# A gated attention and expert-bias block: two buffers for the turned score blocks, the router's rows turned on TensorE, x moved in halves from ScalarE's queue

## The reference, cut to what matters

```python
x = x + tanh(g_xattn) * xattn(_layernorm(x), ctx, mask, Wq, bq, Wk, bk, Wv, bv, Wo, bo)
x = x + tanh(g_ffn)   * ffn(_layernorm(x), router_weight, router_bias, expert_bias)
# xattn: x is (8, 512, 2048); each batch is cut along s into 16 patches of 512 x 128
q, k = Wq @ patch(ln(x)) + bq, Wk @ patch(ln(x)) + bk      # 256 x 128 per patch
v    = Wv @ patch(ctx) + bv
attn = softmax(q_h^T k_h / sqrt(32) masked)                # 8 heads, 128 x 128 each
out  = (Wo @ gelu(attn v^T) + bo) * mask
# ffn: rows t of 2048 features, 64 experts
scores = softmax(flat @ router_weight^T + bias); keep the 8 largest, w_dense
out = flat * sum(kept) + w_dense @ expert_bias
```

## Time and profile before

| | |
|---|---|
| time, median of 3 runs | 1323.04 us (1320.9 to 1323.36) |
| profiled execution, its own time | 1328.39 us |
| its span | 1326.4 us |
| mean granted TensorE clock | 0.963 |
| busy: PE, DVE, ACT, POOL | 85%, 73%, 76%, 66% of the span |
| DMA traffic | 232.27 MB, mean 175 GB/s |

### The profile page before, as it was taken

The page is one execution under the profiler, slowest core; times in us unless marked ns, Lnnn a source line. Parts: engine busy times, 40 slices in busy tenths (PEclk is TensorE's granted clock), DMA queues, the critical chain, the costliest instruction groups (busy, mean ns, idle before and its releaser), DMA issues.

```text
span 1326.4 us, 32364 instructions
## 1 busy us (share of the span) xinstructions
PE 1123.9 (85%) x11165; PEld 1010.7 (76%) x11165; DVE 968.2 (73%) x1859; ACT 1004.8 (76%) x3072; POOL 871.4 (66%) x784
## 2 busy tenths in 40 slices
PE   3779899888898888897888899898989879889857
PEld 3668788878887777787877788787878778878745
DVE  6647768877589766888578876788658876688546
ACT  4767788877789588787879778887778858888743
POOL 2457778567785577856776678756777557775631
PEclk9899999999999899999999999989999989999979
DMA  9395555796557955588656966579555795557543
GB/s 275 105 209 143 137 139 144 182 291 154 143 138 215 259 131 144 141 268 214 147 140 145 290 182 149 135 194 281 144 144 137 229 250 132 143 135 220 138 109 127
DMA packets 169763, 232.27 MB, mean 175 GB/s; under 512 B 27776, under 2 KB 104704, under 8 KB 169472
## 3 DMA queue, kind: packets, MB, share of 16 engines
q1 hardware_dynamic: 168736, 230.19, 66.3%
q10 hardware_dynamic: 864, 0.01, 0.0%
HBM read 80.06 MB, written 33.65 MB: 86 GB/s over the span
## 4 chain that ended last, share of the span: by engine, by line
SPq 36%; DVE 18%; PE 12%; DMA 10%; ACT 10%; issue 9%; POOL 5%; DVEq 0%; ACTq 0%; POOLq 0%
SPq L551 33%; DMA PT<-T 8%; ACT P L643 7%; DVE T L797 5%; DVE T L806 2%; POOL ht_lo L1118 2%; DVE X L936 2%; DVE o L812 2%; DVE nmx L790 2%; DMA cx<-in_ctx 1%; ACT L643 1%; PE ring L475 1%; SPq L556 1%; PE ring L343 1%; DVE bnst L946 1%
## 5 line engine op out<-in xcount | busy, mean ns | idle before, releaser
L643 ACT ACTIVATE P<-ring,nmx 128x128 f32<-128x128 f32 x1024 | 360.6, 389 | 2.1 <-DVE nmx L790 1.3
L328 PE MATMUL ring<-z_hi,wqk_hi 128*128 128x256 f32 x1024 | 302.1, 295 | 24.8 <-DVE z_lo L1000 21.1
L329 PE MATMUL ring<-z_hi,wqk_lo 128*128 128x256 f32 x1024 | 294.3, 287 | 0.0
L330 PE MATMUL ring<-z_lo,wqk_hi 128*128 128x256 f32 x1024 | 294.1, 287 | 0.0
L797 DVE STREAM_TRANSPOSE T<-P 128x512 f32<-128x512 f32 x256 | 170.8, 687 | 135.9 <-DMA PT<-T 134.9
L1106 POOL TENSOR_TENSOR X<-X,xt 128x512 f32<-128x512 f32 x128 | 165.2, 1291 | 153.1 <-DVE xt L825 152.1
L1118 POOL TENSOR_TENSOR ht_lo<-PT,ht_hi 128x512 fp32r<-128x512 f32 x124 | 160.1, 1292 | 133.7 <-ACT ht_hi L667 133.5
L643 ACT ACTIVATION_READ_ACCUMULATOR P<-ring,nmx 128x1 f32 x1024 | 234.5, 229 | 0.0
L328 PEld LDWEIGHTS ring<-z_hi,wqk_hi 128*128 128x128 f32 x1024 | 200.9, 196 | 38.9 <-DVE wqk_lo L975 21.1
L643 ACT ACT_TABLE_LOAD x62 | 79.5, 1283 | 171.0 <-DVE nmx L790 171.0
L825 DVE SCALAR_TENSOR_TENSOR xt<-ring,cst,mg 128x256 f32<-128x256 f32 x256 | 111.5, 477 | 131.3 <-PE ring L405 131.0
(11 more groups left out here) (139 smaller groups left out, 2806.9 us busy)
## 6 DMA issues: line engine op xcount, KB each, us to landing
PT<-T SPq DMA_DIRECT2D x992, 112.0 KB, 2.3
cx<-in_ctx SPq DMA_DIRECT2D x128, 256.0 KB, 3.8
out_y<-X SPq DMA_DIRECT2D x128, 256.0 KB, 4.4
X<-in_x SPq DMA_DIRECT2D x112, 256.0 KB, 4.9
mg<-in_mask SPq DMA_DIRECT2D x64, 128.0 KB, 3.8
X<-in_x SPq DMA_DIRECT2D x8, 512.0 KB, 7.5
sel<-rows_d SPq DMA_DIRECT2D x256, 3.0 KB
PT<-T SPq DMA_DIRECT2D x32, 80.0 KB, 2.6
```

Of the source, the lines that this page charges most:

```text
L328: e.matmul(o, wqk_hi[:, t, cols], z_hi[:, t, :], t == 0, False)
L329: e.matmul(o, wqk_lo[:, t, cols], z_hi[:, t, :], False, False)
L330: last = e.matmul(o, wqk_hi[:, t, cols], z_lo[:, t, :], False, t == DT - 1)
L643: last = e.activation(P[:, n, :], bank("S", 4 * u + g)[:, k * W:(k + 1) * W], ACT.Exp, bias=nmx[u % 2][:, n:n + 1], accum_out=den[u % 2][: ...
```

## The change

It does five things. T becomes two buffers of 20 blocks and PT one of 20; `turn_p(u)` and `turn_d(u)` wait for the moves of u-2 to have landed instead of u-1, and `move(u)` no longer waits for anything of the router. For all units X is turned by `r_turn` on TensorE into two PSUM banks; `r_high` copies from there (ScalarE) and `r_low` subtracts on VectorE; GpSimd has no part in it. `o32` has two buffers, not three. Loads and stores of x are 512 KB (half a tile), 8 and 8 per batch, issued by ScalarE between its activations; only batch 1's first load (16 of 256 KB) and the last batch's stores stay on SP. The tail of a batch is no longer put off by `late` (14.75 slots), and every slot is new.

```diff
-    rows=-11.5, z32=-25.5, z_hi=-20, z_lo=-14.75, q=-14.5, q_ev=-5.25, k=-11, k_ev=-7.5,
-    S=-1.25, top=4, exp=3.5, e_gap=0.25, tp=7, td=7.75, mv=7.25, PV=20, on=23.5,
-    mix=43, m_gap=0.75,
...
+    rows=-26, z32=-25.25, z_hi=-16.75, z_lo=-21.25, q=-12.5, q_ev=-1.75, k=-9, k_ev=-6.75,
+    S=-0.75, top=3.5, exp=4, e_gap=0.25, tp=6.25, td=8, mv=8.75, PV=21.5, on=23.5,
+    mix=42.25, m_gap=0.25,
+    sx=44, sx_gap=1, x2=43.25, st=45.25, st_gap=0.75, rl=50, rl_gap=3.5,
...
-        NC, NV, NR, NO = 2, 4, 7, 3
+        NC, NV, NR, NO = 2, 4, 7, 2
...
-        T = sb("T", [128, 4, 28, 32])
-        PT = sb("PT", [128, 4, 28, 32])
+        T = [sb(f"T{i}", [128, 4, 20, 32]) for i in range(2)]
+        PT = sb("PT", [128, 4, 20, 32])
...
                 for a in range(2):
                     for u in units(t, "hT", C["hT_gap"] * a):
-                        if u >= TF0:
-                            r_turn(u, a)
-                    for u in due(t, C["t_R"] + C["t_gap"] * a, count=TF0):
+                        r_turn(u, a)
+                    for u in units(t, "R", C["hT_gap"] * a):
                         r_mm(u, a)
...
                 if u:
                     e.wait_ge(on_v, u)
-                if u > HLAG:
-                    e.wait_ge(htlo_g, 2 * (u - HLAG))
-                n = 28 if u >= HLAG else 20
-                if u >= HLAG:
-                    e.wait_ge(turn_v, u - HLAG + 1)
                 for b in range(4):
                     for a in range(4):
-                        e.dma_start(PT[32 * b:32 * b + 32, a, 0:n, :], T[32 * a:32 * a + 32, b, 0:n, :]).then_inc(pt_in, 16)
+                        e.dma_start(PT[32 * b:32 * b + 32, a, :, :], T[u % 2][32 * a:32 * a + 32, b, :, :]).then_inc(pt_in, 16)
...
         @block.scalar
         def _(e):
+            def store(b, t, h):
+                e.wait_ge(x2_v, (b * DT + t) * 4 + 2 * h + 2)
+                e.dma_start(ov[b, t, :, h * 1024:(h + 1) * 1024], X[b % 2][:, t, h * 1024:(h + 1) * 1024]).then_inc(out_done[t], 16)
+
+            def load_x(b, t, h):
+                e.wait_ge(out_done[t], out_value(b - 2))
+                e.dma_start(X[b % 2][:, t, h * 1024:(h + 1) * 1024],
+                            xv[b, t, :, h * 1024:(h + 1) * 1024]).then_inc(x_in[b % 2][t], 16)
...
-                if u < TF0:
-                    e.wait_ge(pt_in, 256 * (u + HLAG + 1))
-                    e.activation(by_block(ht_hi[a][:]), turned(a), ACT.Copy).then_inc(hthi_a, 1)
-                else:
-                    e.wait_ge(ht_pe, n - 2 * TF0 + 1)
-                    e.activation(by_block(ht_hi[a][:]), blocks(bank("hT", n)[:]), ACT.Copy).then_inc(hthi_a, 1)
+                e.wait_ge(ht_pe, n + 1)
+                e.activation(ht_hi[a][:], bank("hT", n)[:], ACT.Copy).then_inc(hthi_a, 1)
...
             def turn_p(u, g):
-                if u:
-                    e.wait_ge(pt_in, 256 * u)
+                if u >= 2:
+                    e.wait_ge(pt_in, 256 * (u - 1))
...
-            def turn_h(u):
-                e.wait_ge(pt_in, 256 * (u + HLAG))
-                b, c = divmod(u, NU)
-                e.wait_ge(x1_g, 2 * (u + 1))
-                e.transpose(T[:, :, 20:28, :].rearrange("p q (w t) i -> p w q t i", w=2),
-                            X[b % 2][:, :, c * U:(c + 1) * U].rearrange("p t (w q i) -> p w q t i", w=2, q=4)).then_inc(turn_v, 1)
-
             def r_low(u, a):
                 n = 2 * u + a
...
+                e.tensor_tensor(ht_lo[a][:], bank("hT", n)[:], f32(ht_hi[a][:]), ALU.subtract).then_inc(htlo_v, 1)
```

More of the change, by code:

```diff
@@ L235, in batch @@
             return due(t, 128 + lag, 128, NB)
-        def after(t, lag):
-            return due(t, 128 + lag + C["late"], 128, NB - 1) + tuple(b for b in due(t, 128 + lag, 128, NB) if b == NB - 1)
         def o_parts(u):
@@ L290, in gated_block_kernel @@
                 for u in units(t, "hT", C["hT_gap"] * a):
-                    if u >= TF0:
-                        take(("hT", 2 * u + a), t, end("ht_lo", u) - end("hT", u), htlo_v, 2 * (u - TF0) + a + 1)
-            for b in after(t, C["LT"]):
+                    take(("hT", 2 * u + a), t, end("ht_lo", u) - end("hT", u), htlo_v, 2 * u + a + 1)
+            for b in batch(t, C["LT"]):
                 take(("LT", b), t, C["c_top"] - C["LT"], lg_v, b + 1)
-            for b in after(t, C["wT"]):
+            for b in batch(t, C["wT"]):
                 take(("wT", b), t, C["wt_lo"] - C["wT"], wtlo_v, b + 1)
             for i in range(16):
-                for b in after(t, C["mix"] + C["m_gap"] * i):
+                for b in batch(t, C["mix"] + C["m_gap"] * i):
                     take(("mix", b * 16 + i), t, C["x2"] - C["mix"], x2_v, b * 16 + i + 1)
@@ L593, in _ @@
                 for i in range(16):
-                    for b in after(t, C["x2"] + C["m_gap"] * i):
-                        store(b, i // 4, i % 4)
-                    for b in after(t, C["rl"] + C["rl_gap"] * i):
-                        if b + 2 < NB:
-                            load_x(b + 2, i // 4, i % 4)
+                    for b in batch(t, C["x2"] + C["m_gap"] * i):
+                        if b == NB - 1:
+                            store_last(i // 4, i % 4)
                 for i in due(t, C["x_1"], C["x_gap"], 16):
@@ L603, in _ @@
                         e.wait_ge(v_m, V_SW)
-                    load_x(1, i // 4, i % 4)
+                    load_x1(i // 4, i % 4)
             for t in range(DT):
@@ L675, in c_logits @@
                 e.wait_ge(r_pe, 2 * NU * (b + 1))
-                e.activation(blocks(L[:]), by_block(PR[:]), ACT.Copy).then_inc(l_a, 1)
+                e.activation(L[:], PR[:], ACT.Copy).then_inc(l_a, 1)
             def c_exp(b):
@@ L760, in _ @@
                 for a in range(2):
-                    for u in due(t, C["t_hi"] + C["t_gap"] * a, count=TF0):
+                    for u in units(t, "ht_hi", C["hT_gap"] * a):
                         r_high(u, a)
-                    for u in units(t, "ht_hi", C["hT_gap"] * a):
-                        if u >= TF0:
-                            r_high(u, a)
-                for b in after(t, C["L"]):
+                for b in batch(t, C["L"]):
                     c_logits(b)
-                for b in after(t, C["c_exp"]):
+                for b in batch(t, C["c_exp"]):
                     c_exp(b)
-                for b in after(t, C["wt_hi"]):
+                for b in batch(t, C["wt_hi"]):
                     w_high(b)
                 for i in range(DT):
-                    for b in after(t, C["sx"] + C["sx_gap"] * i):
+                    for b in batch(t, C["sx"] + C["sx_gap"] * i):
                         scale_x(b, i)
+                for i in range(8):
+                    for b in batch(t, C["st"] + C["st_gap"] * i):
+                        if b < NB - 1:
+                            store(b, i // 2, i % 2)
+                    for b in batch(t, C["rl"] + C["rl_gap"] * i):
+                        if b + 2 < NB:
+                            load_x(b + 2, i // 2, i % 2)
         @block.vector
@@ L1066, in _ @@
                     w_low(b)
-                for b in after(t, C["c_sc"]):
+                for b in batch(t, C["c_sc"]):
                     if b < NB - 1:
@@ L1157, in _ @@
                         add_x(u, j)
-                for a in range(2):
-                    for u in due(t, C["t_lo"] + C["t_gap"] * a, count=TF0):
-                        r_low(u, a)
                 for b in batch(t, C["norm2"]):
```

84 lines of the change are left out of this document (27 added, 57 removed), and 10 rows, old and new, of the table ENDS.

## The result

The changed kernel takes 1314.5 us (median of 4 runs, 1311.48 to 1316.57), the one before 1323.2 us beside it (1320.9 to 1323.88): the ratio is 0.9935, 95% interval 0.9912 to 0.9959. It is faster by 0.7%, 8.7 us, where 22 us were forecast. The profiled execution took 1316.57 us, with a span of 1314.7.

The account below looks back on a forecast made before the run. A ring of dependences, with one buffer T waiting for landings, bounded the kernel. After the change a batch takes 8 x 17.3 + 15.0 = 153.4 against 156.2 us; over 7.9 batches 22 us less, so 1301 us, range 1252 to 1340.

Parts of the forecast that it names:

- The ordinary unit: Any unit outside a batch's tail, timed between neighbouring units' moves: 17.9 us before, forecast 17.3 us after the change.
- the ring that was named: Chain through four engines from one unit's `o_high` to the next one's, with half of `project_out` added: 17.3 us.
- The other ring, of PT: Single buffer PT: issues, landing, `weigh`, `divide`, reciprocal and turn of the denominators, put at 16.1 us a unit, not deciding.
- Turns of X on TensorE, cost nothing: Eight transposes a unit start within 0.84 us; TensorE busy 16.5 us, under 17.3, so cost nothing.
- Rival D: Slower by TensorE: transposes take 0.275 us each, 17.9 us a unit, 158.2 a batch, 1339 us; chance 0.07.
- Router's parts, SP, third buffer: VectorE gains two subtractions, at most 11.1 us busy, covered; SP's ctx load and the third `o32` buffer cost 0.
- Smaller moves cost or gain nothing: Moves of 20 instead of 28 blocks: 16 issues keep their price; a shorter landing gains at most a few tenths.
- The tail unit: The one unit into which a batch's whole tail falls: 30.6 us between maxima, 13.3 over an ordinary unit.
- rival C: Slower by ScalarE's queue in the tail unit: issues about 1.1 us instead of 0.48, 159 a batch, 1345 us; chance 0.17.
- The tail's 1.7 us for what comes later: Estimate added to the tail's 13.3: seven later loads on ScalarE (0.5), base terms on VectorE (about 0.7), statistics (0.5).
- The base: Time of a whole batch before the change, from moves eight units apart: 156.19 us.
- Rival A: Faster by much: unit 16.6 us, about TensorE's own work, tail 14, 146.8 a batch, 1249 us; chance 0.22.

## Why the prediction was right and wrong

**The ordinary unit** was right: 17.3 forecast, 17.2 measured, in the ring that was named and with each of its steps within 0.2 us. That this ring decides is shown by taking 1.6 us out of it (16.4 us a unit then). The other ring, of PT, was put at 16.1 us, which was too long: 11.05 for the issues holds the last one, and the 2.26 of its landing are counted from its start, so the same rows make 15.5. Units of 15.8 us in the run with the later half of `project_out` bear that out. It decided nothing here.

**The second T** was given the fall from 17.9, and that is not what the runs show. With one T the unit is 17.2 as well, and also with moves of the old width. The prediction had the turn of X in the old ring and did not ask what that ring would be without it. So 17.3 was right as the ring that decides, but it would have been right without the second buffer too.

**Turns of X on TensorE, cost nothing**: right, and twice as many are hidden in an ordinary unit too. TensorE is busy 16.0 us there, 16.5 were forecast. Rival D is refuted. In TensorE's timeline of the changed kernel, and in its groups of instructions (busy us, mean ns of one), they stand so, as in the earlier trace rows:

```profile
478.64 1.04 PE L402 MATMUL ring<-ident,X 128*128 128x128 f32 x8
...
479.43 0.36 PE L323 MATMUL ring<-wv_hi,cx_hi 128*128 128x256 f32 x1
```

```profile
L402 PE MATMUL ring<-ident,X 128*128 128x128 f32 x512 | 68.4, 277 | 0.5 <-POOL X L1069 0.5
```

Eight begin within 0.79 us. The Trainium skill's 275 ns ("TensorE: Matmul & The Clock Gate", "Part 4: PE-mode transpose") and our 0.10 us are both true: the groups of instructions give one transpose a mean of 277 ns, the time from its start to its end, while the next starts 0.1 us after it.

**Router's parts, SP, third buffer**: VectorE is busy 10.5 to 12.7 us in ordinary units, where "at most 11.1" was given. The row behind that bound, 9.78 us, was a unit with few statistics: its neighbour took 11.92 us. It is still covered.

**Smaller moves cost or gain nothing** is true of the ordinary unit and false of the tail. Wide moves with one T make a batch 8 us dearer there, where one T alone adds nothing. The forecast looked for a price on the issue, and there is little; the price is on the landing, beside other traffic.

**The tail unit** was right: 30.0 for 30.6 us. ScalarE's last three issues ahead of its exponentials took 1.13 to 1.20 us each, more than the 0.8 from which rival C was to decide. But the exponentials' table load began 0.85 us behind the maxima (559.04 against 558.19), where 0.77 is usual (475.72 against 474.95), so the two were level and C did not come about. The sign of being wrong that was put on those issues came true all the same: the nine issues took 7.7 us in all, where the sum had 4.4, and part of them ran beside activations.

**The tail's 1.7 us for what comes later** is the step that failed. It held 0.5 us for the loads: one issue between exponentials and Gelu. On the mean of six batches the two periods of the tail unit stand 14.0 us above two ordinary ones, and those behind it another 6.1, in sum 20 us where the forecast had 15.0. Without the bytes of the loads it is 14.1 and 0.4. The loads cost 5.6 us a batch, not by their issues but by the landing of the moves beside which they run. The prediction said that no landing gets faster; it never asked whether one gets slower, though it moved 4 MB a batch to an engine whose free moment is exactly SP's busiest. A batch without them is 152.0 us, under the 153.4 forecast; with them it is 157.6. Six batches make 25.5 us.

**The base** was off by 1.1 us: 156.19 came from one pair of moves, and the mean of six batches is 157.3. That gives back 6.6 of those 25.5 us, and the 18.9 left are what the six batches miss of their forecast (16.8 gained, 2.1 lost). The first and last batches, to which the sum gave the remaining 5.2 us, gained 8.6 and 2.0, and the end, which it left alone, 2.9. Without these the change would have gained nothing in the profiled execution.

Of the rule on issuing engines ("DMA: Bandwidth & Descriptors", "Issuing engines are not separate DMA queues" in the Trainium skill) the runs agree: 1283.4 us with the loads on SP and 1283.8 on ScalarE's queue, at moments that are both free. The prediction took from it only that no landing gets faster. The same rule says that DMAs of all issuing engines interleave on the same DMA engines. This case shows what that costs: loads on ScalarE's queue made the last of SP's moves land after 7.9 us.

**Rival A**, 1249 us, was ruled out for the change as made; two sets of slots away its time is there, at 1243. It comes from other parts than the rival had: 16.4 us a unit and a tail of 15.9, where 16.6 and 14 were named.

## What to carry to other kernels

When a transfer moves to another queue, look up what the first queue is doing at that moment, and above all who waits for the last of a series: bytes ahead of the first of 16 moves cost nothing here, the same bytes beside the last cost 5.6 us a batch. A slot in a table is a place in an engine's order, and the time at which it comes is read from the trace: what stands behind a waiting instruction goes out all at once when it ends. Take the period of a loop from several of its turns, not from one.

## What the runs showed of the hardware

- Beside four loads of 512 KB (DMA share 1.02, 323 GB/s) a move of 80 KB landed 7.9 us after its issue, where 2.2 is the median; the same bytes in pieces of 256 KB left the time of the kernel as it was (1314.1 us).
- DMA issues on ScalarE go beside its running activations: at 569.07 a load is issued (0.35 us) while `o_high` runs from 568.87 to 569.50. Three of them ahead of the Gelu left the period at 17.3 us.
- TensorE idle for most of 8 us came back at a clock of 0.50, and matmuls then started 0.21 us apart where 0.12 is usual. In units with eight and with sixteen transposes the granted clock stayed 1.00.
